# A two-layer graph network on one core: layer 2's aggregation with the features as the stationary operand, and layer 1's multiply, bias and relu one batch of builds later

## The reference, cut to what matters

```python
src, dst, norm = _gcn_norm(edge_index, num_nodes)      # adds loops, norm = dinv[src] * dinv[dst]
def _gcn_layer(x, W, b, src, dst, norm, num_nodes):
    h = x @ W
    msg = h[src] * norm[:, None]
    agg = jax.ops.segment_sum(msg, dst, num_segments=num_nodes)
    return agg + b
z = relu(_gcn_layer(xn, W1, b1, ...))
z = relu(_gcn_layer(z, W2, b2, ...))
x = x + z + mix(xn)                                    # then x + ffn(layernorm(x))
```

## Time and profile before

| | us |
|---|---|
| median of 3 runs | 2124.17 (2123.45 to 2128.42) |
| the profiled execution | 2122.97 |
| its span, first to last instruction | 2121.1 |
| PE busy | 1900.7 (90% of the span) |
| DVE busy | 1179.8 (56%) |
| ACT busy | 878.9 (41%) |
| POOL busy | 289.1 (14%) |
| mean granted PE clock | 0.951 |

### The profile page before, as it was taken

One profiled execution on the slowest core, in us unless ns is written; L12 is line 12 of the kernel. 1 busy time (PEld: TensorE's weight loads), 2 busy tenths in 40 slices (PEclk: granted clock), 3 DMA queues, 4 the chain that ended last, 5 costly groups with the idle time before them and its releaser, 6 DMA issues. The chain is left out here.

```text
span 2121.1 us, 37341 instructions
## 1 busy us (share of the span) xinstructions
PE 1900.7 (90%) x11735; PEld 1126.4 (53%) x11735; DVE 1179.8 (56%) x2764; ACT 878.9 (41%) x1997; POOL 289.1 (14%) x418
## 2 busy tenths in 40 slices
PE   3069997969999999999999799999999999999588
PEld 3045555845555555555555445555555555555477
DVE  6368872255666656566666235555555555555422
ACT  2157770035555555555555323333333333333200
POOL 3502222310000000000000200000000000000033
PEclk7579998989999999999999999999999999999789
DMA  3113325922222222222222344334343434342078
GB/s 92 31 43 112 111 98 180 285 81 107 107 91 121 91 121 91 116 96 102 110 91 121 120 152 141 141 134 148 127 154 123 156 123 156 125 146 102 20 235 249
DMA packets 106576, 262.52 MB, mean 124 GB/s; under 512 B 15682, under 2 KB 73386, under 8 KB 93978
## 3 DMA queue, kind: packets, MB, share of 16 engines
q1 hardware_dynamic: 76245, 225.23, 29.8%
q10 hardware_dynamic: 28116, 32.06, 4.3%
q0 software_dynamic: 2176, 4.75, 0.8%
HBM read 138.39 MB, written 124.42 MB: 124 GB/s over the span
## 5 line engine op out<-in xcount | busy, mean ns | idle before, releaser
L1344 PE MATMUL ps<-hs,at 128*128 128x512 f16 x2401 | 670.5, 378 | 3.3 <-POOL at L1261 3.3
L1539 PE MATMUL ps<-big,at 128*128 128x512 f16 x2401 | 559.7, 380 | 5.9 <-DMA at<-at_scratch 5.9
L1391 ACT CAST at<-ps 128x392 f16<-128x392 f32 x784 | 375.0, 486 | 430.3 <-PE ps L1333 408.4
L1333 PE MATMUL ps<-big 128*128 128x98 f16 x3136 | 465.0, 209 | 11.2 <-DVE big L1289 11.2
L1333 PEld LDWEIGHTS ps<-big 128*128 128x128 f16 x3136 | 298.4, 98 | 151.4 <-issue 10.8
L1539 PEld LDWEIGHTS ps<-big,at 128*128 128x128 f16 x2401 | 233.5, 98 | 255.6 <-issue 10.5
L1344 PEld LDWEIGHTS ps<-hs,at 128*128 128x128 f16 x2401 | 229.9, 97 | 146.3 <-POOL at L1261 3.5
L1289 DVE TENSOR_TENSOR big<-big,key_lo 128x1024 f16<-128x1024 f16 x392 | 268.5, 685 | 0.0
L1289 DVE TENSOR_TENSOR big<-big,key_hi 128x784 f16<-128x784 f16 x392 | 219.6, 560 | 17.5 <-POOL big L1251 7.6
L1751 POOL TENSOR_TENSOR key_lo<-key_lo,big 128x512 f32<-128x512 f32 (+1 forms) x49 | 61.8, 1262 | 708.0 <-ACT big L1713 708.0
L1300 DVE TENSOR_TENSOR big<-ps,big 128x256 f32<-128x256 f32 x49 | 20.8, 425 | 208.4 <-ACT big L1399 208.4
(11 more groups left out here) (275 smaller groups left out, 2218.4 us busy)
## 6 DMA issues: line engine op xcount, KB each, us to landing
at_scratch<-at SPq DMA_DIRECT2D x49, 1568.0 KB, 5.2
at<-at_scratch SPq DMA_DIRECT2D x49, 1568.0 KB, 6.5
xT_scratch<-big SPq DMA_DIRECT2D x98, 128.0 KB, 1.8
big<-xT_scratch SPq DMA_DIRECT2D x49, 256.0 KB, 3.5
wT_scratch<-big ACTq DMA_DIRECT2D x49, 256.0 KB, 2.1
hs<-wT_scratch SPq DMA_DIRECT2D x49, 256.0 KB, 3.4
big<-in_x_dram SPq DMA_DIRECT2D x96, 128.0 KB, 2.5
base_scratch<-big ACTq DMA_DIRECT2D x48, 128.0 KB, 4.1
```

Source lines behind the costliest of these rows:

```text
L1333: te.matmul(ps[:, BANKS[i // UW % len(BANKS)], i % UW * KC:(i % UW + 1) * KC], lhsT=hot_lo[:, s, :].rearrange("p (q k r) -> p q k r", k=P, ...
L1344: mm = te.matmul(ps[:, 2 + b, :], lhsT=at[:, b, k * P:(k + 1) * P], rhs=hs[:, k, :], start=(k == 0), stop=(k == T - 1))
L1391: a.copy(to.rearrange("p k (i j) -> p k i j", j=WIN), ps[:, BANKS[m % len(BANKS)], 0:UW * KC].rearrange("p (i k j) -> p k i j", i=UW, j=WI ...
L1539: mm = te.matmul(ps[:, b, :], lhsT=at[:, b, k * P:(k + 1) * P], rhs=hs2[:, k, :], start=(k == 0), stop=(k == T - 1))
```

## The change

In layer 1 three places in the written-out order move: PE's `multiply` from i = 28 to 36, DVE's `bias` from batch 5 to 6, ACT's `relu` from store 12 to 13. In layer 2 the operands of the aggregation change places: the stationary operand is a 128-column block of `hs2` (two blocks of the high half, two of the low), the moving one the 128x128 block of `at`. Four matmuls of 128 columns stand for one of 512. High and low parts accumulate into the same PSUM columns, and the result is already transposed, channels by nodes. So `turn`, `gather`, the copy `low` and their buffers and semaphores go, ACT copies PSUM straight into `aggT`, `multiply` moves from k = 12 to k = 6, and DVE's loop has no lead any more.

```diff
--- before.py
+++ after.py
@@ -1314,7 +1314,7 @@
                             hots(t + 1, i)
                         if i == 2 and reached(t, 1):
                             gather(t - 1, 1 - b)
-                        if i == 5 and reached(t, 1):
+                        if i == 6 and reached(t, 1):
                             bias(t - 1, 1 - b)
 
                 pipeline(dve, tile, T, 2, lead=1, lag=1)
@@ -1369,7 +1369,7 @@
                             aggregate(t, b, range(i * (T - ALONE) // WPT, (i + 1) * (T - ALONE) // WPT))
                         if i == 20 and reached(t, 1):
                             turn(t - 1, 1 - b)
-                        if i == 28 and reached(t, 1):
+                        if i == 36 and reached(t, 1):
                             multiply(t - 1, 1 - b)
                     if reached(t, 0) and within(t, T):
                         aggregate(t, b, range(T - ALONE, T))
@@ -1421,7 +1421,7 @@
                             lows(t - 1, 1 - b)
                         if m == 6 and reached(t, 1):
                             keep(t - 1, 1 - b)
-                        if m == 12 and reached(t, 1):
+                        if m == 13 and reached(t, 1):
                             relu(t - 1, 1 - b)
 
                 pipeline(act, tile, T, 2, lead=1, lag=1)
@@ -1479,8 +1479,6 @@
         WS = 2.0 ** 15
         with ExitStack() as stage:
             take = carve(big_f[:, T * C:])
-            agg = take([P, 2, C])
-            low = take([P, 2, C])
             aggT = take([P, 2, CB, NT])
             zb = take([P, 2, C])
             base_in = take([P, 2, C])
@@ -1502,8 +1500,7 @@
             w2_loaded = sem("w2_loaded")
             at_loaded, base_loaded = [sem(f"l2_at_loaded{b}") for b in range(2)], [sem(f"l2_base_loaded{b}") for b in range(2)]
             x1_out, w_out = [sem(f"x1_out{b}") for b in range(2)], [sem(f"w_out{b}") for b in range(2)]
-            summed, low_ready, agg_ready = sem("l2_summed"), sem("l2_low_ready"), sem("l2_agg_ready")
-            agg_turned, aggT_ready, multiplied = sem("l2_agg_turned"), sem("l2_aggT_ready"), sem("l2_multiplied")
+            summed, aggT_ready, multiplied = sem("l2_summed"), sem("l2_aggT_ready"), sem("l2_multiplied")
             x1_ready, ln_step, xn2_ready = sem("x1_ready"), sem("l2_ln_step"), sem("xn2_ready")
             xn2_turned, xn2T_ready, logits_ready = sem("xn2_turned"), sem("xn2T_ready"), sem("logits_ready")
             shifted, exp_ready, soft_step, w_ready = sem("shifted"), sem("exp_ready"), sem("soft_step"), sem("w_ready")
@@ -1535,17 +1532,14 @@
                     if k == 0:
                         pe.wait_ge(at_loaded[b], 16 * u + 16)
                         if reached(t, 2):
-                            pe.wait_ge(agg_ready, t - 1)
-                    mm = te.matmul(ps[:, b, :], lhsT=at[:, b, k * P:(k + 1) * P], rhs=hs2[:, k, :],
-                                   start=(k == 0), stop=(k == T - 1))
+                            pe.wait_ge(aggT_ready, t - 1)
+                    for h in range(2):
+                        for c in range(CB):
+                            mm = te.matmul(ps[:, b, c * NT:(c + 1) * NT], lhsT=hs2[:, k, h * C + c * P:h * C + (c + 1) * P],
+                                           rhs=at[:, b, k * P:(k + 1) * P], start=(k == 0 and h == 0 and c == 0),
+                                           stop=(k == T - 1 and h == 1), skip_group_check=True)
                     if k == T - 1:
                         mm.then_inc(summed, 1)
-
-                def turn(t, b):
-                    pe.wait_ge(agg_ready, t + 1)
-                    for c in range(CB):
-                        mm = te.transpose(ps[:, 2, c * NT:(c + 1) * NT], agg[0:NT, b, c * P:(c + 1) * P], ident[0:NT, 0:NT])
-                    mm.then_inc(agg_turned, 1)
 
                 def multiply(t, b):
                     pe.wait_ge(aggT_ready, t + 1)
@@ -1595,7 +1589,7 @@
                         if reached(t, 0) and within(t, T):
                             sum_tile(t, b, u, k)
                         if reached(t, 1) and within(t, T + 1):
-                            for at_k, do in ((6, turn), (12, multiply), (31, turn_x), (37, logits)):
+                            for at_k, do in ((6, multiply), (31, turn_x), (37, logits)):
                                 if k == at_k:
                                     do(t - 1, 1 - b)
                         if k == 44 and reached(t, 2):
@@ -1611,10 +1605,6 @@
             @block.vector
             def _(dve):
                 v = nc.vector
-
-                def gather(t, b):
-                    dve.wait_ge(low_ready, t + 1)
-                    v.tensor_tensor(agg[0:NT, b, :], ps[0:NT, b, 0:C], low[0:NT, b, :], ALU.add).then_inc(agg_ready, 1)
 
                 def norm(t, b, u):
 
@@ -1678,13 +1668,10 @@
                         norm(t, b, u)
                         shift(t, b)
                         divide(t, b)
-                    if within(t, T - 1):
-                        gather(t + 1, 1 - b)
-                    if reached(t, 0):
                         split(t, b)
 
                 dve.wait_ge(w2_loaded, 32)
-                pipeline(dve, tile, T, 2, lead=1)
+                pipeline(dve, tile, T, 2)
                 dve.wait_ge(s_added, T)
                 v.tensor_scalar(s_sum.rearrange("p a b -> p (a b)"), ps[:, 6:8, :].rearrange("p a b -> p (a b)"),
                                 1.0 / WS, None, ALU.mult)
@@ -1694,9 +1681,9 @@
                 a = nc.scalar
                 def rest(t, b):
                     act.wait_ge(summed, t + 1)
-                    a.copy(low[0:NT, b, :], ps[0:NT, b, C:2 * C]).then_inc(low_ready, 1)
-                    act.wait_ge(agg_turned, t + 1)
-                    a.copy(aggT[:, b].rearrange("p a b -> p (a b)"), ps[:, 2, 0:CB * NT]).then_inc(aggT_ready, 1)
+                    if reached(t, 2):
+                        act.wait_ge(multiplied, t - 1)
+                    a.copy(aggT[:, b].rearrange("p a b -> p (a b)"), ps[:, b, 0:CB * NT]).then_inc(aggT_ready, 1)
                     act.wait_ge(ln_step, 2 * t + 2)
                     a.activation(rstd[0:NT, b:b + 1], mv[0:NT, b, 1:2], ACT.Sqrt, bias=eps[0:NT, 0:1]).then_inc(std_ready, 1)
                     act.wait_ge(xn2_turned, t + 1)
```

## The result

| | before, us | after, us |
|---|---|---|
| median | 2124.04 (4 runs, 2123.45 to 2128.42) | 2075.26 (4 runs, 2074.43 to 2075.95) |
| profiled execution | 2122.97 | 2074.43 |
| span | 2121.1 | 2072.6 |

A forecast was written before the change was run, and what follows sets the result against it. PE's issue and waits were taken to bound both loops. From the profiled 2122.97 us, layer 1's 38.4 and layer 2's 9.5 came off: 2075.1, on the median 2076; own range 2064 to 2094, eight in ten 2064 to 2116.

The forecast's parts named there:

- PE's time sets both loops: Both layer loops: PE is busy 96% and 99%, so a microsecond saved in a tile counts once per tile, 49 times.
- Layer 1, 0.80 us a tile, 38.4 us: Layer 1's multiply: 0.86 us of wait for the copy of keep goes, 0.06 of exposed load stays; 48 tiles.
- The margins for DVE, ACT and POOL: Layer 1 after the moves: copy done 0.7 us before PE arrives, hots covered by 1.6, self_loops by 0.8.
- Rival 1: Layer 1: the wait only moves, to DVE or POOL; only layer 2's 9.5 us are gained, 2115 us; chance 0.06.
- The pair of load and matmul costs 0.056 us: Layer 2's new aggregation: pace from eight weigh pairs; four against 0.2156 give +0.0084 us per k, +0.41 per tile.
- rival 3: Layer 2's sum_tile: loads bind in a long run, slower; gain gone at 0.061 us a pair, 2431 at L457's pace; chance 0.10.
- the far bound: Upper bound for a layer-2 pair: L457's unbroken run of 105 small matmuls in 9.94 us, 0.093 each, loading 112 columns.
- Layer 2, 0.15 us a tile and 9.5 us in all: Layer 2: -0.61 + 0.41 + 0.05 per tile, -7.2 us; with edges -0.9, -1.8 and +0.4; ends -24 and +5.
- What goes: Layer 2's turn: 0.61 us a tile, 0.34 of wait for DVE's gather and 0.27 of its own.
- what comes: Layer 2, per tile: +0.41 us for four pairs per k, +0.05 for the multiply's float32 load.
- Rival 2: Layer 2's two-tile body, 460 pairs, leaves PE's instruction store: 37 to 75 us more, 2113 to 2151; chance 0.05.
- `norm` perhaps a little late: Layer 2, DVE: norm may start a little late, but its output leaves 1.6 us of room before turn_x.

The follow-up runs named there:

- the two halves measured alone: Layer 1's three moves alone, layer 2 as before: 2086.7 us; layer 2's new aggregation alone, layer 1 as before: 2112.21 us.
- at i = 35: Changed kernel with layer 1's multiply at i = 35 in place of 36, behind an aggregation and not a build: 2073.37 us, ratio 0.9765.
- the half-column kernel: Changed kernel with every layer-2 block loaded twice, 64 moving columns each time, 392 pairs a tile: 2108.83 us, one run.

## Why the prediction was right, step by step

- **PE's time sets both loops, a microsecond counts once a tile.** Shown: the two halves measured alone give 37.4 and 11.9 us, which add up to the whole.
- **Layer 1, 0.80 us a tile, 38.4 us.** The tile went from 15.41 to 14.62 us, 0.79 less, and the layer from 754.0 to 716.3, 37.7 less. The 0.06 us of exposed load are there (0.92 for the multiply), and gone at i = 35. The margins for DVE, ACT and POOL held: PE is busy in 595.00 of 595 us, and even with `bias` and `relu` in their old places nothing waits. Rival 1 is refuted.
- **The pair of load and matmul costs 0.056 us.** Measured 0.0559 over a hundred. This was the term that everything in layer 2 hung on, taken from one row of eight; that a burst's pace would hold in a long run was a choice, with rival 3 at 0.10 against it. Rival 3 is refuted with its condition: the half-column kernel keeps hiding loads at 0.0292 us a pair, so the load binds nowhere near 0.061. L457's 0.093, the far bound, is another shape's. The Trainium skill's figure of about 81 ns for a sustained stream at N=128 (TensorE: Matmul & The Clock Gate, Back-to-back issue gap) is not what these runs show; here the measurement decides, and its isolated gap of about 56 ns is the sustained one too.
- **Layer 2, 0.15 us a tile and 9.5 us in all: too small by 2.5.** The tile went from 15.33 (44 tiles from the `turn` at 1277.96 to that at 1952.55) to 15.14, 0.19. What goes was read rightly: over 40 tiles of the trace of the kernel before, the wait in front of `turn` is 0.34 us on average and `turn` itself 0.27. So what comes costs 0.61 - 0.19 = 0.42 and not 0.46. With 0.05 for the multiply's load, 0.37 is left for 49 k, which is a pair of 0.0558; the price of 0.056, from a row of 0.45 us for eight, was a little high. 0.04 x 48 is 2 us. The rest is at the end of the layer: the multiply now starts at 1918.61, 0.7 us after the last pair (1917.9), and started 2.95 after the last sum before. That is 2.2 less where 1.8 was expected. ACT's copy starts 0.3 us after the last pair (1918.19); the 0.70 that the prediction put there was read in the middle of the loop.
- **The loop's body stays in the instruction store.** No gap in the loop with 460 pairs, and none after the first pass with 852. The instruction queue's packets grew with the pairs that stand in the code. Rival 2 is refuted for these sizes. The Trainium skill's 2048 instructions for PE (Runtime: NRT & Kernel Launch, Instruction fetch mechanics) agree with it: 1704 loads and matmuls a pass ran without refetch. What happens above that was not tried.
- **DVE's slack in front of `norm` in layer 2 nearly goes and costs nothing.** The prediction had `norm` perhaps a little late. It isn't: DVE ends its last work at 1496.69 and still waits 0.23 us for the multiply. Its output is done at 1485.16 in the tile before, 1.9 us ahead of turn_x at 1487.06; 1.6 was expected:

```profile
1484.74 0.42 DVE L1634 TENSOR_TENSOR big<-big 128x256 f16<-128x256 f32 x1
...
1496.00 0.69 DVE L1664 TENSOR_TENSOR big<-big 128x512 f16<-128x512 f32 x1
1496.92 0.48 DVE L1612 SCALAR_TENSOR_TENSOR big<-ps,dun,key_hi 128x256 f32<-128x256 f32 x1 [0.23 <-PE ps L1547]
```

That the forecast of 2076 came within 1 us of 2075.26 is in part luck: layer 1 gave 0.7 us less than its term, layer 2 2.5 more, and the rest of the kernel, of which nothing was said, took 1.2 more.

What the prediction didn't ask is whether each part could be had more cheaply. Its own numbers said so: `turn` was 0.34 of wait and 0.27 of work, the new blocks cost 0.46, so of the 0.61 the wait was all that was worth removing. (Without the wait `turn` costs even less, 0.22: as I read it, its own float32 load then hides behind the aggregation in front.)

## What to carry to other kernels

Where an engine works in order through a hand-written order and is the bound, look for an operation placed right behind the one that its input's copy waits for; moving it later by as much other work as it waited for is the whole gain, and the neighbours' moves may not be needed. Before restructuring an operation to get rid of it, split its cost into wait and work: a wait can often be had by one changed number. Swapping stationary and moving operands at equal columns costs here only the fixed 2.5 ns of each extra matmul (2 x 29.2 - 55.9, from the half-column kernel). It lost in layer 1, where the transpose was on time. In layer 2, where the transpose waited, it gained, but moving the transpose gained more. So it is worth its price only where such a wait can't be had by another place in the order; no run here shows such a case.

## What the runs showed of the hardware that was not expected

- A 128x128 f16 load, recorded at 98 ns, hides behind a matmul of 64 columns: 200 pairs at 0.0292 us each. The recorded duration of a load is not its pace.
- At that pace PE stood still five times in the first six tiles of the layer, up to 1.3 us each and 4.1 us in sum, always in code that ran for the first time, and never in the 21 later passes of the same loop. At 0.0559 us a pair there is none, also where the instruction queue moves as many packets (38, the kernel with blocks in layer 1). I read it as PE waiting for its instructions, since the releaser is `issue`; it was not tested apart, and two tiles of new code ran without it.
- A float32 load that nothing covers costs 0.10 us, behind a build of 98 columns 0.06, behind a pair of 128 columns 0.05, behind 512 columns nothing.
